# Self attention of a four layer block: the order of scores, constant products, transposes, maxima and copies, and four small steps on GpSimd

## The chip, the cores and the metric

One core of a Trainium2 chip runs the whole program; the other cores are idle. The metric is device time in microseconds (us) of one execution. The engines are TensorE (PE), VectorE (DVE), ScalarE (ACT), GpSimd (POOL) and SyncE (SP), which only issues transfers here.

## The reference

Four layers follow each other on tokens x of shape (4, 256, 256); each is a cross attention on a context of 64 positions and then an FFN block, both added to x. The FFN block of the third layer (called 2 in the kernel) begins with a self attention of its own, and that is the part the change touches. In short, with n the layer norm of x, and dropping biases and the rotation's tables:

```python
q, k, v = heads(rms(n) @ wq + bq), heads(rms(n) @ wk + bk), heads(rms(n) @ wv + bv)   # 16 heads of 16
q, k = rope(q, k)
scores = where(causal, einsum('bqhd,bkhd->bhqk', q, k) / 4, -inf)
attn = softmax(scores, axis=-1)
n = n + einsum('bhqk,bkhd->bqhd', attn, v) @ wo
h = rms(n)                                    # router, experts and shared FFN follow
x = x + n + ffn(h)
```

## The kernel before

x lies in SBUF as eight tiles of 128 tokens (two per batch), and so does n (`xn`). Every engine has its own written-out queue; semaphores tie them together (`s.p` is the exponentials, `s.pt_ps` the transposes, `s.pt` their copies, `s.mx` the maxima, `s.one` the inverses of the sums spread over a head's columns, `s.oneT_ps` their transposes, `s.o` the normalised context, `s.y_ps` its product with wo). `me.link` is an increment of VectorE's own semaphore followed by a wait for it.

The self attention is `pe_self`, `act_self`, `dve_self` and the second half of `pool_pre2`. It has 32 steps (`SA_STEPS`): eight query tiles (`bq`), and in each four steps of four heads. An even query tile sees 128 keys, an odd one 256. For a step t:

- `pe_scores(t)` (L2222) waits for the exponentials of step t-2, whose banks it takes over, and makes the mask (L2232) and the three f16 products (L2242) of four heads.
- `dve_maxima(t)` (L2102, L2106) reduces them to negated maxima; `act_self` (L2337) makes the exponentials with their sums, four instructions.
- `turned(t)` of `pe_self` (L2249) waits for the copy of step t-1, then for some steps issues products of constants whose result nobody reads (`pe_warm`, L306: three at t % 4 = 2, four at t = 1 and 4), then waits for the exponentials of t and transposes them (L2259, four or eight). All steps use the same two PSUM banks.
- `turned(t)` of `dve_self` (L2353) copies them to SBUF.
- `values` (L2276) multiplies them with v, two steps at a time.

Once per query tile there are the reciprocals of the sums (L2359), their spreading to 256 columns (L2360), the transposes of that (`sums_transposed`, L2284), its evacuation on ScalarE (L2329), the multiplication of the context by it (`normalised`, L2367), the product with wo (`project`, L2290), the addition to n (L2373), the addition of n to x (L2374) and the sum of squares (L2375). The layer norm of one tile (`dve_normed`, L1899) is also one VectorE instruction of this loop. GpSimd does nothing in the loop and two powers (L1857) behind it.

The order of the main loops is:

```python
# pe_self                          # dve_self
turned(t)                          reciprocals if t % 4 == 3
pe_scores(t + 2)                   turned(t)
values(t - 2) if t even            dve_maxima(t + 2)
sums_transposed if t % 4 == 0      dve_normed if t % 4 == 1
project if t % 4 == 3              normalised if t % 4 == 2, added if t % 4 == 0
# act_self: exponentials(t); sums_evacuated if t > 4 and t % 4 == 1
```

Of the kernel before, what the change touches and what calls it, by code (L numbers as in the profile page):

```python
# [16 lines left out]
ALU, ACT, AX = mybir.AluOpType, mybir.ActivationFunctionType, mybir.AxisListType  # L17

P = 128
D = 256  # L20
KT = D // P
B, S, L = 4, 256, 64
NT = B * S // P
QT = S // P
# [68 lines left out]
def build(nc, d, out):  # L93
    ctx = ExitStack()
    with ctx:
# [98 lines left out]
        def bank(n, k=1):  # L194
# [18 lines left out]
               2: Sems("att2", "bt_ps bt e_ps e m_ps mh m f_ps f c_ps c dt_ps dt q s")}  # L213
        pre = [Sems("pre0", "fold_ps fold ms r z zT_ps zT biased y_ps ssq rr z2 z2T_ps h low"),
               Sems("pre1", "h low logit e t"),
               Sems("pre2", "hT z zT_ps ms r qkv biased copied qr qrT_ps qhi qT s mx p pt_ps pt one oneT_ps oneT v pv o y_ps x2 "
                    "ssq rr z2 z2T_ps h low logit e t"),
               Sems("pre3", "h low logit lg t")]
        ffn = Sems("ffn", "up0 up1 dn0 dn1 up_hi up_lo dn_hi dn_lo parts gates_ps gates rows gate0 gate1 "
# [1444 lines left out]
        def dve_ffn(n, begun=0):  # L1664
            dve, s, f = nc.vector, ffn, FFNS[n]
            LAG = lag(n)

            def low(st):
                dve.wait_ge(s.hi, f.steps0 + place(n, st) + 1)
                if gated(n, st):  # L1670
                    dve.tensor_tensor(hid_part(n, 1, st), m_b[:, st % PRODUCTS, :], hid_part(n, 0, st), ALU.subtract).then_inc(s.lo, 1)  # L1671
                else:
                    dve.scalar_tensor_tensor(hid_part(n, 1, st), m_b[:, st % PRODUCTS, :], plain_down_scale(n, st), hid_part(n, 0, st),
                                             ALU.mult, ALU.subtract).then_inc(s.lo, 1)

            for st in range(f.steps + LAG - 2):
                c, h, due = st // 2, st % 2, finished(n, st)
                if len(due) == 2:
                    if due[0] % 2 == 0:
                        dve_dn_lo(n, due[0] // 2)  # L1680
                    low(due[0])
                if begun <= st < f.steps:
                    dve_front(n, st)
                if h == 0 and 2 <= c + 1 < f.tiles:
                    dve_up_lo(n, c + 1)
                if due and due[-1] % 2 == 0:
                    dve_dn_lo(n, due[-1] // 2)
                if st < f.steps and product_first(n, st):
                    dve.wait_ge(s.t, f.steps0 + st + 1)
                    dve.scalar_tensor_tensor(m_b[:, st % PRODUCTS, :], m_t[:, h, :], 1.0, m_a[:, h, :], ALU.add, ALU.mult).then_inc(s.prod, 1)  # L1690
                if due:
                    low(due[-1])
                if n == 0:
                    dve_routed(own["dve"], st)
            for i in range(NT):
                dve.wait_ge(s.y_ps, NT // 2 * n + i // 2 + 1)
                dve.scalar_tensor_tensor(x[:, i, :], PS[:, 4 + i // 2, (i % 2) * D:(i % 2 + 1) * D],
                                         UNDOWN if n else p0_down[:, i:i + 1], x[:, i, :], ALU.mult, ALU.add).then_inc(ffn_x, 1)
                if n == 2:
                    dve_stats(2 * n + 2, i)  # L1700
            if n == 1:
                for i in range(NT):
                    dve_stats(2 * n + 2, i)
# [542 lines left out]
        def pe_self():  # L2246
            pe, s = nc.tensor, pre[2]

            def turned(t):  # L2249
                b, q, j0, keys = sa_part(t)  # L2250
                if t:
                    pe.wait_ge(s.pt, t)
                    if t % SA_OF_Q == 2 or t in (1, 4):
                        pe_warm(3 if t % SA_OF_Q == 2 else 4, 2)
                pe.wait_ge(s.p, t + 1)
                for e in range(2):
                    for a in range(2):
                        for k in range(q + 1):
                            ins = pe.transpose(PS[:, 2 + e, (a * (q + 1) + k) * P:(a * (q + 1) + k + 1) * P],  # L2259
                                               sa_p[:, t % 2, e, a * keys + k * P:a * keys + (k + 1) * P], ident[:])  # L2260
                ins.then_inc(s.pt_ps, 1)

            def values(t):

                b, q, j0, keys = sa_part(t)
                bq = t // SA_OF_Q
                pe.wait_ge(s.pt, t + 2)
                if j0 == 0:
                    pe.wait_ge(s.v, b + 1)
                    if bq >= 2:  # L2270
                        pe.wait_ge(s.x2, bq - 1)
                for a in range(2):
                    for k in range(q + 1):
                        for j in range(j0, j0 + 4):
                            out_ps = PS[32 * (j % 4):32 * (j % 4) + 32, 6 + q, (j // 4) * P:(j // 4 + 1) * P]
                            ins = pe.matmul(out_ps, sa_vm[b][:, k, j, a, :, :].rearrange("p e c -> p (e c)"),  # L2276
                                            turned_part(t + (j - j0) // 2)[:, j % 2, (a * (q + 1) + k) * P:(a * (q + 1) + k + 1) * P],
                                            start=(a == 0 and k == 0), stop=(a == 1 and k == q))
                ins.then_inc(s.pv, 2)

            def sums_transposed(bq):
                pe.wait_ge(s.one, bq + 1)
                for g in range(G):
                    ins = pe.transpose(PS[:, 6 + bq % QT, D + g * P:D + (g + 1) * P], sa_one[:, g * P:(g + 1) * P], ident[:])  # L2284
                ins.then_inc(s.oneT_ps, 1)

            def project(bq):
                pe.wait_ge(s.o, bq + 1)
                for g in range(G):
                    ins = pe.matmul(PS[:, 6 + bq % QT, 0:D], sa_oT[:, bq % QT, g, :], p2_wo[:, g, :], start=(g == 0), stop=(g == G - 1))  # L2290
                ins.then_inc(s.y_ps, 1)

            for t in range(1, SA_AHEAD):
                pe_scores(t)
            for t in range(SA_STEPS):
                turned(t)
                if t + SA_AHEAD < SA_STEPS:
                    pe_scores(t + SA_AHEAD)
                if t and t % 2 == 0:
                    values(t - 2)  # L2300
                if t and t % SA_OF_Q == 0:
                    sums_transposed(t // SA_OF_Q - 1)
                if t >= SA_OF_Q and t % SA_OF_Q == 3:
                    project(t // SA_OF_Q - 1)
            values(SA_STEPS - 2)
            sums_transposed(B * QT - 1)
            pe_warm(6, 2)
            project(B * QT - 1)

        def pool_values(me):  # L2310
# [4 lines left out]
            for i in range(NT):  # L2315
# [5 lines left out]
                if k == QT - 1:  # L2321
                    ins.then_inc(s.v, 1)

        def act_self():
            act, s = nc.scalar, pre[2]

# [4 lines left out]
            for t in range(SA_STEPS):  # L2331
                b, q, j0, keys = sa_part(t)
                act.wait_ge(s.mx, t + 1)
                for e in range(2):
                    for a in range(2):
                        h = 2 * (j0 + e) + a
# [8 lines left out]
        def dve_self(me):  # L2345
# [8 lines left out]

            def reciprocals(bq):
                dve.wait_ge(s.p, SA_OF_Q * (bq + 1))
                if bq:
                    dve.wait_ge(s.oneT_ps, bq)
                me.link(dve, dve.reciprocal(small[:, bq % QT, 2, :], small[:, bq % QT, 1, :]))  # L2359
                dve.tensor_copy(sa_one.rearrange("p (h c) -> p h c", h=H), over(small[:, bq % QT, 2, :], 2, HD)).then_inc(s.one, 1)  # L2360

            def normalised(bq):
# [7 lines left out]
            def added(bq):  # L2370
                dve.wait_ge(s.y_ps, bq + 1)
                dve.wait_ge(ln.xn, 5 * NT + bq + 1)
                me.link(dve, dve.tensor_tensor(xn[:, bq, :], xn[:, bq, :], PS[:, 6 + bq % QT, 0:D], ALU.add))  # L2373
                dve.tensor_tensor(x[:, bq, :], x[:, bq, :], xn[:, bq, :], ALU.add).then_inc(s.x2, 1)  # L2374
                ins = dve.scalar_tensor_tensor(p2_junk, xn[:, bq, :], 1.0, xn[:, bq, :], ALU.mult, ALU.mult,  # L2375
                                               accum_out=p2_ssq[:, bq:bq + 1])
                me.link(dve, ins)
# [9 lines left out]
            for t in range(1, SA_AHEAD):  # L2387
                dve_maxima(t)
            for t in range(SA_STEPS):
                if t % SA_OF_Q == SA_OF_Q - 1:  # L2390
                    reciprocals(t // SA_OF_Q)
                turned(t)
                if t + SA_AHEAD < SA_STEPS:
                    dve_maxima(t + SA_AHEAD)
                if t % SA_OF_Q == 1:
                    dve_normed(5, t // SA_OF_Q)
                if t >= SA_OF_Q and t % SA_OF_Q == 2:
                    normalised(t // SA_OF_Q - 1)
                if t >= 2 * SA_OF_Q and t % SA_OF_Q == 0:
# [37 lines left out]
        def pool_pre2():  # L2437
# [1 line left out]
            pool_ln(5)  # L2439
            me = own["pool"]  # L2440
            pool_values(me)
            for part in range(2):
                pool_pow(pre[2].ssq, part + 1, rms_r[:], rms_e[:], pre[2].rr, part)

        def dve_pre2():
            dve, s, me = nc.vector, pre[2], own["dve"]
# [265 lines left out]
```

## Time and profile before

| what | value |
|---|---|
| median of 3 runs | 1248.03 us (1244.47 to 1248.77) |
| the profiled execution | 1244.87 us |
| its span | 1242.8 us |
| PE, DVE, ACT, POOL busy | 95%, 74%, 41%, 32% |
| granted clock of TensorE over the span | 0.999 |
| self attention, scores of step 1 to last product with wo | 747.52 to 835.99 us |

The profile is one execution, taken by the hardware profiler. The span runs from its first to its last instruction. A record's length is start to end; instructions of one engine overlap, so the distance from start to start can be shorter than a record. Some matmul records are missing. "idle before <- releaser" in square brackets is the time in which the engine waited ahead of this record, and what ended the wait.

### The profile page before, as it was taken

Reading aid. Unit: us, or ns where it says so; the run is one execution under the profiler, and the core shown is the slowest. Engines: PE = TensorE matmul, PEld = TensorE weight load, DVE = VectorE, ACT = ScalarE, POOL = GpSimd, SP = SyncE. Lnnn points to the kernel's source line nnn. Section 1 sums busy time; section 2 is a strip of 40 time slices with the busy share of each in tenths; the row PEclk is TensorE's granted clock in tenths of the full one; section 3 lists DMA queues with packets and bytes.
Section 4 is the critical chain, followed back from the end, with each engine's and each line's share of the span. In section 5 each row is a group of like instructions: output and inputs, shape, how many; then the busy total and the mean of one; then the engine's idle time right before and its main releaser. Section 6 shows DMA issues by size and latency. Waiting matters only on the chain.

```text
span 1242.8 us, 21905 instructions
## 1 busy us (share of the span) xinstructions
PE 1179.6 (95%) x8530; PEld 768.3 (62%) x8559; DVE 917.5 (74%) x1718; ACT 505.3 (41%) x1141; POOL 393.2 (32%) x397
## 2 busy tenths in 40 slices
PE   6999999999999999999999989899999988999998
PEld 3664658999745555555766745564566665455556
DVE  3777976677677777778757798887866577777766
ACT  3523360111224333334453336653434353555553
POOL 1540215656305333334003330001534052433330
PEclk9999999999999999999999999999999999999999
DMA  4040141000065344443240000002532100533431
GB/s 150 2 161 22 49 148 39 1 1 2 5 218 161 119 119 119 116 117 105 94 150 1 3 15 1 2 1 60 168 128 92 61 19 1 151 113 113 123 119 56
DMA packets 41542, 97.18 MB, mean 78 GB/s; under 512 B 5446, under 2 KB 18246, under 8 KB 39392
## 3 DMA queue, kind: packets, MB, share of 16 engines
q1 hardware_dynamic: 41440, 95.79, 24.4%
q8 instruction: 68, 1.11, 0.4%
q14 instruction: 34, 0.28, 0.1%
HBM read 94.35 MB, written 1.42 MB: 77 GB/s over the span
## 4 chain that ended last, share of the span: by engine, by line
PE 76%; DVE 15%; issue 3%; ACT 3%; DMA 2%; POOL 1%; SPq 0%; DVEq 0%; ACTq 0%; POOLq 0%
PE PS L1461 9%; PE PS L1463 9%; PE PS L1462 9%; PE PS L1508 5%; PE PS L1510 5%; PE PS L1509 5%; PE PS L1074 3%; PE PS L1092 2%; PE PS L1271 2%; PE PS L306 2%; PE PS L1060 2%; PE PS L1062 2%; PE PS L1061 2%; PE PS L2259 1%; DVE small L577 1%
## 5 line engine op out<-in xcount | busy, mean ns | idle before, releaser
L1718 POOL TENSOR_TENSOR arena<-arena,m_g 128x512 f32<-128x512 f32 x142 | 196.7, 1406 | 351.6 <-DMA m_g<-gate_rows 344.1
L1461 PE MATMUL PS<-arena 128*128 128x512 f16 x608 | 230.7, 379 | 3.0 <-DVE arena L1656 2.4
L1462 PE MATMUL PS<-arena 128*128 128x512 f16 x608 | 230.7, 379 | 0.0
L1463 PE MATMUL PS<-arena 128*128 128x512 f16 x608 | 230.6, 379 | 0.0
L1508 PE MATMUL PS<-arena 128*128 128x256 f16 x608 | 166.3, 274 | 6.6 <-DVE arena L1671 5.0
L1510 PE MATMUL PS<-arena 128*128 128x256 f16 x608 | 166.3, 274 | 0.0
L1509 PE MATMUL PS<-arena 128*128 128x256 f16 x608 | 166.2, 273 | 0.0
L1611 ACT ACTIVATE arena<-PS 128x512 f32<-128x512 f32 x112 | 66.8, 597 | 226.6 <-PE PS L1463 219.9
L1659 DVE SCALAR_TENSOR_TENSOR arena<-arena,PS 128x512 f32<-128x512 f32 x112 | 76.8, 685 | 77.1 <-ACT arena L1611 75.9
L1671 DVE TENSOR_TENSOR arena<-arena 128x512 f16<-128x512 f32 x142 | 128.5, 909 | 2.2 <-ACT arena L1622 1.8
L1463 PEld LDWEIGHTS PS<-arena 128*128 128x128 f16 x608 | 59.5, 98 | 71.9 <-issue 0.3
L1461 PEld LDWEIGHTS PS<-arena 128*128 128x128 f16 x608 | 59.5, 98 | 63.8 <-DVE arena L1656 3.4
L1462 PEld LDWEIGHTS PS<-arena 128*128 128x128 f16 x608 | 59.5, 98 | 57.9 <-issue 0.2
L1145 POOL TENSOR_TENSOR arena<-arena 128x256 f32<-128x256 f32 x96 | 67.6, 726 | 79.4 <-DVE arena L1175 79.3
L1622 ACT ACTIVATE arena<-arena 128x512 f16<-128x512 f32 x142 | 87.0, 618 | 2.9 <-PE PS L1510 2.9
L1662 DVE TENSOR_TENSOR arena<-arena,PS 128x512 f32<-128x512 f32 x112 | 77.0, 687 | 12.6 <-DVE arena L1659 0.9
L1552 DVE SCALAR_TENSOR_TENSOR arena<-w_stage,arena 128x512 f16<-128x512 f32 x80 | 78.9, 988 | 6.3 <-ACT arena L1547 6.3
L1508 PEld LDWEIGHTS PS<-arena 128*128 128x128 f16 x608 | 59.5, 98 | 36.4 <-issue 8.8
L1509 PEld LDWEIGHTS PS<-arena 128*128 128x128 f16 x608 | 59.6, 98 | 16.9
L306 PE MATMUL PS<-causal_b,ident_b 128*128 128x512 bf16 x246 | 60.0, 379 | 7.2 <-DVE arena L2353 5.7
L1510 PEld LDWEIGHTS PS<-arena 128*128 128x128 f16 x608 | 59.6, 98 | 7.1
L2337 ACT ACTIVATE arena<-PS,arena 128x128 f32<-128x128 f32 (+1 forms) x128 | 52.0, 420 | 21.7 <-DVE arena L2106 21.5
(282 smaller groups left out, 2223.1 us busy)
## 6 DMA issues: line engine op xcount, KB each, us to landing
w_stage<-in_up SPq DMA_DIRECT2D x80, 256.0 KB, 3.0
m_g<-gate_rows SPq DMA_DIRECT2D x70, 256.0 KB, 4.1
arena<-in_heads SPq DMA_DIRECT2D x16, 1088.0 KB, 5.3
w_stage<-in_down SPq DMA_DIRECT2D x80, 128.0 KB, 2.1
m_g<-gate_rows SPq DMA_DIRECT2D x17, 512.0 KB, 4.0
m_g<-gate_rows SPq DMA_DIRECT2D x6, 448.0 KB, 3.9
m_g<-gate_rows SPq DMA_DIRECT2D x6, 384.0 KB, 4.1
m_g<-gate_rows SPq DMA_DIRECT2D x6, 320.0 KB, 4.1
```

Source lines behind the costliest of these rows:

```text
L306: nc.tensor.matmul(PS[:, free, :], ident_b[:], mask_lat, start=True, stop=True)
L1461: pe.matmul(to, w_hi, x_hi, start=(k == 0), stop=False)
L1462: pe.matmul(to, w_lo, x_hi, start=False, stop=False)
L1463: ins = pe.matmul(to, w_hi, x_lo, start=False, stop=(k == KT - 1))
L1508: pe.matmul(to, h_hi, w_hi, start=(c == 0 and i % 2 == 0), stop=False)
L1509: pe.matmul(to, h_hi, w_lo, start=False, stop=False)
L1510: ins = pe.matmul(to, h_lo, w_hi, start=False, stop=(last and i % 2 == 1))
L1552: nc.vector.scalar_tensor_tensor(up_w[:, c % 2, 1, :], up_in[:, c % 2, :], SPLIT, up_w[:, c % 2, 0, :], ALU.mult, ALU.subtract).then_inc(s ...
L1622: act.activation(hid_part(n, 0, st), m_b[:, st % PRODUCTS, :], ACT.Copy).then_inc(s.hi, 1)
L1662: dve.tensor_tensor(m_b[:, st % PRODUCTS, :], a, u_ps, ALU.mult).then_inc(s.prod, 1)
L1671: dve.tensor_tensor(hid_part(n, 1, st), m_b[:, st % PRODUCTS, :], hid_part(n, 0, st), ALU.subtract).then_inc(s.lo, 1)
L1718: pool.tensor_tensor(p, p, m_g[:, st // 2 % 2, st % 2, :], ALU.mult).then_inc(s.c, 1)
```

## The change

```diff
 # pe_self
             for t in range(SA_STEPS):
-                turned(t)
                 if t + SA_AHEAD < SA_STEPS:
                     pe_scores(t + SA_AHEAD)
+                turned(t)
 # values: PSUM banks of tile bq are free again
-                        pe.wait_ge(s.x2, bq - 1)
+                        pe.wait_ge(s.mixed, bq - 1)
 # act_self
                 act.wait_ge(s.mx, t + 1)
+                if t >= 2:
+                    act.wait_ge(s.pt_ps, t - 1)
 # dve_self
             def reciprocals(bq):
                 dve.wait_ge(s.p, SA_OF_Q * (bq + 1))
-                if bq:
-                    dve.wait_ge(s.oneT_ps, bq)
-                me.link(dve, dve.reciprocal(small[:, bq % QT, 2, :], small[:, bq % QT, 1, :]))
+                if bq >= 2:
+                    dve.wait_ge(s.one, bq - 1)
+                ins = dve.reciprocal(small[:, bq % QT, 2, :], small[:, bq % QT, 1, :])
+                if bq < B * QT - 1:
+                    ins.then_inc(s.inv, 1)
+                    return
+                me.link(dve, ins)
+                dve.wait_ge(s.oneT_ps, bq)
+                dve.wait_ge(s.one, bq)
                 dve.tensor_copy(sa_one.rearrange("p (h c) -> p h c", h=H), over(small[:, bq % QT, 2, :], 2, HD)).then_inc(s.one, 1)
             def added(bq):
-                me.link(dve, dve.tensor_tensor(xn[:, bq, :], xn[:, bq, :], PS[:, 6 + bq % QT, 0:D], ALU.add))
-                dve.tensor_tensor(x[:, bq, :], x[:, bq, :], xn[:, bq, :], ALU.add).then_inc(s.x2, 1)
+                dve.tensor_tensor(xn[:, bq, :], xn[:, bq, :], PS[:, 6 + bq % QT, 0:D], ALU.add).then_inc(s.mixed, 1)
+                dve.wait_ge(s.mixed, bq + 1)
             for t in range(SA_STEPS):
+                if t + SA_AHEAD < SA_STEPS:
+                    dve_maxima(t + SA_AHEAD)
                 if t % SA_OF_Q == SA_OF_Q - 1:
                     reciprocals(t // SA_OF_Q)
                 turned(t)
-                if t + SA_AHEAD < SA_STEPS:
-                    dve_maxima(t + SA_AHEAD)
-                if t % SA_OF_Q == 1:
-                    dve_normed(5, t // SA_OF_Q)
 # pool_pre2: the two powers are now inside pool_self
+        def pool_self():
+            pool, s = nc.gpsimd, pre[2]
+            def normed(i):
+                pool.wait_ge(ln.rstd, powers_before[5] + 1)
+                pool.tensor_scalar(xn[:, i, :], x[:, i, :], meanvar[:, i, 0:1], rstd[:, i:i + 1],
+                                   ALU.subtract, ALU.mult).then_inc(ln.xn, 1)
+            def spread(bq):
+                pool.wait_ge(s.inv, bq + 1)
+                if bq:
+                    pool.wait_ge(s.oneT_ps, bq)
+                pool.tensor_copy(sa_one.rearrange("p (h c) -> p h c", h=H), over(small[:, bq % QT, 2, :], 2, HD)).then_inc(s.one, 1)
+            def added(bq):
+                pool.wait_ge(s.mixed, bq + 1)
+                pool.tensor_tensor(x[:, bq, :], x[:, bq, :], xn[:, bq, :], ALU.add).then_inc(s.x2, 1)
+            normed(0)
+            for bq in range(B * QT - 1):
+                normed(bq + 1)
+                spread(bq)
+                if bq:
+                    added(bq - 1)
+            pool_pow(s.ssq, 1, rms_r[:], rms_e[:], s.rr, 0)
+            added(B * QT - 2)
+            pool_pow(s.ssq, 2, rms_r[:], rms_e[:], s.rr, 1)
+            added(B * QT - 1)
 # end of the FFN of layer 2, ahead of its additions to x
+            if n == 2:
+                dve.wait_ge(pre[2].x2, NT)
```

Two semaphores are new, `inv` and `mixed`. No arithmetic changes.

## Rows read from the trace of the kernel before

**Rows 1.** Stretches: length, busy us of PE, PEld, DVE, ACT, POOL; granted clock, DMA.
```profile
747.52:763.68 16.16, 15.01 (x134) 7.97 (x137) 12.01 (x16) 10.57 (x50) 0.00 (x0) 1.00 0.01 2
785.12:806.57 21.45, 19.67 (x226) 12.64 (x227) 19.04 (x33) 14.38 (x66) 0.00 (x0) 1.00 0.01 2
828.01:836.00 7.99, 6.69 (x93) 4.70 (x92) 6.68 (x18) 2.31 (x9) 1.33 (x1) 1.00 0.01 2
```
**Rows 2.** Waits in 785.12 to 806.57 us: total us, times, longest us.
```profile
ACT arena L2337 <- DVE arena L2106: 5.5, 5, 1.6
...
PE PS L306 <- DVE arena L2353: 1.5, 2, 1.1
```

**Rows 3.** Timeline of TensorE: start us, length us, instruction.
```profile
784.69 0.59 PE L306 MATMUL PS<-causal_b,ident_b 128*128 128x512 bf16 x2 [1.09 <-DVE arena L2353]
785.12 1.04 PE L2259 MATMUL PS<-ident,arena 128*128 128x128 f32 x8
785.99 0.38 PE L2232 MATMUL PS<-causal_b,ident_b 128*128 128x256 bf16 x2
...
786.74 1.08 PE L2276 MATMUL PS<-arena 128*32 128x128 f32 x32
787.75 1.09 PE L2259 MATMUL PS<-ident,arena 128*128 128x128 f32 x8
...
789.42 1.13 PE L2290 MATMUL PS<-arena 128*128 128x256 f32 x4
790.39 0.60 PE L2259 MATMUL PS<-ident,arena 128*128 128x128 f32 x4
790.83 0.38 PE L2232 MATMUL PS<-causal_b,ident_b 128*128 128x256 bf16 x2
...
801.00 0.82 PE L2242 MATMUL PS<-arena 32*128 32x512 f16 x6
...
802.08 0.65 PE L2276 MATMUL PS<-arena 128*32 128x128 f32 x16
802.65 0.44 PE L2284 MATMUL PS<-ident,arena 128*128 128x128 f32 x2
802.93 1.04 PE L2259 MATMUL PS<-ident,arena 128*128 128x128 f32 x8
```

**Rows 4.** Timeline of VectorE.
```profile
788.88 1.22 DVE L2353 COPY arena<-PS 128x1024 f32<-128x1024 f32 x1
790.02 0.68 DVE L2106 TENSOR_REDUCE arena<-PS 128x4 f32<-128x512 f32 x1
...
792.74 0.43 DVE L2374 TENSOR_TENSOR x<-x,xn 128x256 f32<-128x256 f32 x1
...
794.75 0.40 DVE L1899 TENSOR_SCALAR xn<-x,meanvar,rstd 128x256 f32<-128x256 f32 x1
...
798.42 0.29 DVE L2360 COPY arena<-small 128x256 f32<-128x256 f32 x1
```

**Rows 5.** Timeline of ScalarE.
```profile
785.57 0.47 ACT L2337 ACTIVATE arena<-PS,arena 128x256 f32<-128x256 f32 x1 [1.59 <-DVE arena L2106]
...
787.29 0.21 ACT L2337 ACTIVATION_READ_ACCUMULATOR arena<-PS,arena 128x1 f32 x1
788.05 0.37 ACT L2337 ACTIVATE arena<-PS,arena 128x128 f32<-128x128 f32 x1 [0.55 <-DVE arena L2106]
...
789.34 0.21 ACT L2337 ACTIVATION_READ_ACCUMULATOR arena<-PS,arena 128x1 f32 x1
...
793.05 0.38 ACT L2329 ACTIVATE arena<-PS 128x256 f32<-128x256 f32 x1 [0.81 <-PE PS L2284]
```

**Rows 6.** Min/median/max ns of a line: L1867, L1899 near 81 us, L1659.
```profile
L1867 POOL TENSOR_TENSOR arena<-xn,arena x8: 722/910/916, 81.6 to 87.6; 128x256 f32<-128x256 f32 x8
L1899 DVE TENSOR_SCALAR xn<-x,meanvar,rstd x8: 406/952/959, 81.1 to 86.1; 128x256 f32<-128x256 f32 x8
L1659 DVE SCALAR_TENSOR_TENSOR arena<-arena,PS x112: 673/686/690, 101.9 to 1223.0; 128x512 f32<-128x512 f32 x112
```

More of the change, by code:

```diff
@@ L215, in build @@
                Sems("pre1", "h low logit e t"),
-               Sems("pre2", "hT z zT_ps ms r qkv biased copied qr qrT_ps qhi qT s mx p pt_ps pt one oneT_ps oneT v pv o y_ps x2 "
+               Sems("pre2", "hT z zT_ps ms r qkv biased copied qr qrT_ps qhi qT s mx p pt_ps pt inv one oneT_ps oneT v pv o y_ps mixed x2 "
                     "ssq rr z2 z2T_ps h low logit e t"),
@@ L2441, in pool_pre2 @@
             pool_values(me)
-            for part in range(2):
-                pool_pow(pre[2].ssq, part + 1, rms_r[:], rms_e[:], pre[2].rr, part)
+            pool_self()
         def dve_pre2():
```

## The prediction, made before the changed kernel was run

> **What bounds the kernel now.** The page's shares say only that TensorE is nearly always busy. The change touches one stage, the self attention of the third FFN layer, so the view that counts is busy time by stretch [rows 1]. The stage runs from 747.52 us (scores of step 1) to 835.99 us (last product with wo), 88.47 us or 7% of the span of 1242.8. It settles into a period of eight steps (two query tiles, one with 128 keys, one with 256): three of them, 21.44 to 21.45 us (one stands). In a period TensorE is busy 19.7 us, VectorE 19.0, ScalarE 14.4, GpSimd 0. Two engines are close to full and a third is in a loop with them, so what decides is who waits for whom. The waits [rows 2]: ScalarE waits 5.5 us a period for maxima, TensorE 1.5 us for copies of transposed probabilities (that wait stands in front of the constant products, L306).
>
> For the replay below I read occupied times as start to next start. TensorE [rows 3]: eight transposes 0.87 (785.12 to 785.99; elsewhere up to 1.0, I take 0.93), four transposes 0.44 (790.39; up to 0.59 elsewhere, I take 0.48), scores of a 128 key step 0.75 (785.99 to 786.74), of a 256 key step 1.07 to 1.08 (801.00 to 802.08), values 1.01 (786.74) or 0.57 (802.08), sums 0.27 (802.65), product with wo 0.97 (789.42), three constant products 0.65 (three at 0.215, the first of the three at 784.47 has no record). Over a period: 4 x 0.93 + 4 x 0.48 + 4 x 1.07 + 4 x 0.75 + 2 x 1.01 + 2 x 0.57 + 2 x 0.27 + 2 x 0.97 + 2 x 0.65 = 19.85. So TensorE stands idle 1.6 us a period; before steps 14 and 22 about 1.1 us of it in one piece. VectorE [rows 4]: copies and maxima 1.14 (256 keys) or 0.61 (128). ScalarE [rows 5]: a step's exponentials take 1.93 us from the first start to the last end for 256 keys (785.57 to 787.50) and 1.50 for 128 (788.05 to 789.55), eight records each, the first and the last of which stand; the evacuation of the sums (793.05) holds the queue 0.28 us. From a producer's end to the consumer's start: 0.04 us to VectorE, 0.03 to ScalarE, 0.06 to 0.13 to TensorE. Putting the queues of lines 2293 to 2304, 2331 to 2343 and 2387 to 2400 in their order with these times gives a period of 21.48 us and a stage of 88.46 us, against 21.44 and 88.47 in the trace; so I use the same table for the new order.
>
> **What GpSimd takes over.** Per tile VectorE loses the normalisation (0.41 us record, 0.33 occupied), the spreading of the inverses (0.29, some 0.21 to 0.34 with the wait behind the reciprocal) and the addition to x (0.43, 0.35 occupied) [rows 4]: 0.9 to 1.0 us a tile, 7 to 8 us in all. GpSimd gets 8 normalisations, 7 spreads (the eighth stays on VectorE), 8 additions. Its price here is not shown; the nearest row is its addition of 128x256 in the first FFN block, 0.72 to 0.92 us [rows 6]; a normalisation or a broadcast copy may differ. I take 0.9, as bounds 0.7 and twice the row's median, 1.8. Even at 1.8 us the seven spreads come in time: the reciprocal stands at step 4n+3, the transposes of the sums follow a step later, some 3 us on, and GpSimd has three instructions in 10 us. So GpSimd's own work costs nothing while it hides in that slack; without it each spread would add its length in front of a sums transpose. Its last additions stand behind the power that VectorE waits for and are needed only at the end of the FFN, so the new wait for x2 there costs 0. Keeping the old order and moving this work alone, the table gives 87.4 us: only 1.0 us of the 7 to 8 comes off, since TensorE and the loop through it stay.
>
> **The new order.** Scores(t+2) now stand before constants and transposes(t) on TensorE, maxima(t+2) before copy(t) on VectorE, and exponentials(t) wait for transposes(t-2) (the p buffer was guarded by the order before). No instruction is added or taken on TensorE, so its 19.85 us a period remain; only waits can change. Three things follow.
> 1. Scores(t+2) wait for exponentials(t). In the old order the transposes of t, which want the same exponentials, and ahead of them the constant products stood there; the products filled the wait. Now TensorE stands still in front of the scores with everything behind it, and the constant products come afterwards, in series.
> 2. The evacuation of the sums stands on ScalarE's queue ahead of exponentials 4n+2. It already waits 0.81 us for the transposes of the sums [rows 5]. ScalarE is now further ahead of TensorE, so this wait sets its pace. One period from transposes(14) = 0: values and scores(17) to 2.69, transposes(15) to 3.62, product to 4.59, scores(18) 5.34, transposes(16) 5.82, values 6.83, sums to 7.10 (result 7.27); evacuation 7.30, exponentials(18) 7.58 to 9.08; scores(19) and transposes(17) are done at 8.33, so scores(20) wait from 8.33 to 9.21: 0.88 idle. Constants to 10.93, then without a wait transposes(18), values, scores(21), transposes(19), product, scores(22), transposes(20), values and sums to 17.33. Evacuation again, exponentials(22) 17.81 to 19.74; TensorE ends transposes(21) at 19.33 and starts scores(24) at 19.87: 0.54 idle, to 20.62. Maxima(23) start at 18.86 behind the squares, copy(21) at 20.00 and ends at 21.22, so the constants of step 22 start at 21.28: 0.66 idle; transposes(22) at 21.93.
> 3. The period is thus 21.93 us: idle 2.08 against 1.6 before.
>
> **Sum.** Steps 1 to 6 take 18.20 against 16.16 us [rows 1]: 0.75 is scores(8), now ahead of that point, the rest waits, chiefly 1.22 us in front of scores(3), where the four constants of step 1 used to stand. The three periods: 3 x 21.93 - 64.33 = +1.5. The end from step 30: 7.77 against 7.98, -0.2 (the power, the tokens and the last product are in the same order). Together +2.0 + 1.5 - 0.2 = +3.3 us. Behind the stage the ten constants ahead of the logits (ten at 0.215) hide the 0.35 us that the missing addition saves; should they not, the end comes 0.35 us earlier. Contention adds 0 to 2.7 us (next part), I take 0.7: **+4 us**, 0.3%. Changing each time of the table by 0.1 us moves the difference by at most 0.8, so the bounds without contention are +2 and +5.
>
> The profiled execution took 1244.87 us (span 1242.8 and 2.1 around it), so it would be 1248.9; the median of the three runs is 1248.03, 3.2 above it, which would give 1252. I take the middle, 1250.5.
>
> **Contention.** VectorE's normalisation takes 0.40 us in this stage, where GpSimd is idle [rows 4], and mostly 0.95 us in the first FFN block, where GpSimd adds beside it; products with a PSUM operand stay at 0.69 us at the most, GpSimd busy or not [rows 6]. The copies, maxima and the multiplications by inverses read PSUM and are not stretched; the squares (L2375) and reciprocals read SBUF only. Stretched by 0.5 us each, they lengthen the period in the table: 1.5 us over the stage for the squares, 2.7 with the reciprocals and a GpSimd at 1.3 us.
>
> The Trainium skill (Advanced Engine Details and Errata, VectorE Performance Modes) says that VectorE's second SBUF port is shared with GpSimd and that the two block each other in 2-port modes. By that rule the squares, which read one tensor twice, and not the PSUM copies, would pay, as the trace's 0.69 against 0.95 us suggests; it is the third rival below.
>
> **Rivals.**
> - *The waits go and the relief comes through.* If exponentials run ahead as the order means them to, only TensorE's work is left. Ceiling: all idle of the stage, some 7.8 us; 1.0 is what the relief gives alone. Against it: the evacuation on ScalarE's queue. Time -1 to -6, say -3: 1246.5. Chance 0.14, of which 0.05 passes 0.5%.
> - *Nothing to be seen*, -1 to +2: relief and waits cancel, for instance if transposes behind scores run 0.05 us shorter (32 x 0.05 = 1.6). 1248.5. Chance 0.2.
> - *Clearly slower.* GpSimd stretches VectorE's SBUF instructions on the path copy(21), maxima(23): +2.7 on the +3.3, and transposes behind a score product cost 0.05 more each (+1): +7, 1253.5. It decides when squares take over 0.8 us. Chance 0.24.
> - *TensorE's clock drops.* Granted clock is 1.00 (2.4 GHz) in all stretches [rows 1], with pauses up to 1.1 us; the longest new one is 1.95 us, before step 30. A stretch of 3 us at 1.2 GHz would cost 1.5 us. Chance 0.02, in the slower share.
>
> **The numbers.** 0.5%, 6.2 us, is about what a measurement here can tell from no change. The forecast (+2 to +6) holds 0.40; with the second rival and the first's small part the middle has 0.69; faster 0.05; slower 0.26. The range takes the runs' own spread (1244.5 to 1248.8) with -3 and +10: 1242 to 1259.
>
> **What would show it.** Right: a period of about 21.9 us; TensorE waiting 0.9 us in front of scores for exponentials, twice a period; the wait in front of L306 down from 1.1 to about 0.7; ScalarE waiting over 1 us for the sums (0.8 before); VectorE under 17.5 us busy a period; L2375 at 0.42 to 0.9 us. Wrong: a period under 21.2 us, TensorE's waits in front of scores under 0.3 us, or PSUM copies over 1.3 us.

## The result, and the profile after

The changed kernel takes 1250.22 us (median of 17, 1245.77 to 1254.18) against 1245.34 us for the kernel before in the same comparison (1241.97 to 1248.77). The ratio is 1.0035 with a 95% interval of 1.0024 to 1.0046, so +3.0 to +5.7 us. That is a real loss and a small one: within the half per cent that was called no change, and near the forecast of +4.

The profile after has a span of 1248.7 us. Its lines are two further down from L2106 on (maxima L2108, masks L2234, scores L2244, transposes L2261, values L2278, sums L2286, product L2292); copies are L2386, exponentials L2370, the evacuation L2360, the squares L2414. Busy time by stretch, columns as in [rows 1]: steps 1 to 6, one period from transposes(14) to transposes(22), the end from transposes(30), and the whole stage.

```profile
747.59:767.45 19.86, 17.68 (x144) 9.09 (x145) 12.42 (x15) 12.33 (x58) 1.60 (x2) 0.91 0.00 1
789.19:810.92 21.73, 20.05 (x227) 12.70 (x226) 17.11 (x26) 14.17 (x68) 5.12 (x6) 1.00 0.01 2
832.66:840.89 8.23, 6.75 (x93) 4.68 (x91) 5.99 (x15) 0.50 (x3) 2.04 (x2) 1.00 0.01 2
747.59:840.89 93.30, 83.79 (x906) 51.53 (x906) 69.15 (x107) 55.37 (x257) 17.78 (x21) 0.98 0.01 2
```

Against [rows 1]: 19.86 us for 16.16, 21.73 for 21.45, 8.23 for 7.98, and the stage 93.30 for 88.47, +4.8. VectorE has been relieved as intended (17.1 us busy in a period, 19.0 before) and the period is 0.3 us longer all the same. The granted clock of the first stretch is 0.91, which was 1.00; more on that below.

Where TensorE stands still in a period is in its timeline, which answers to [rows 3].

```profile
796.06 0.44 PE L2286 MATMUL PS<-ident,arena 128*128 128x128 f32 x2
...
797.09 0.66 PE L2261 MATMUL PS<-ident,arena 128*128 128x128 f32 x4
798.38 0.82 PE L2244 MATMUL PS<-arena 32*128 32x512 f16 x6 [0.63 <-ACT arena L2370]
...
807.36 1.04 PE L2261 MATMUL PS<-ident,arena 128*128 128x128 f32 x8
808.75 0.39 PE L2234 MATMUL PS<-causal_b,ident_b 128*128 128x256 bf16 x2 [0.34 <-ACT arena L2370]
...
810.27 0.82 PE L306 MATMUL PS<-causal_b,ident_b 128*128 128x512 bf16 x3 [0.70 <-DVE arena L2386]
810.92 1.04 PE L2261 MATMUL PS<-ident,arena 128*128 128x128 f32 x8
```

Three waits: scores(20) 0.63 us and scores(24) 0.34 us for exponentials, the constants of step 22 0.70 us for a copy, 1.67 us in all. The kernel before has three others in the period of [rows 3]:

```profile
794.52 0.59 PE L306 MATMUL PS<-causal_b,ident_b 128*128 128x512 bf16 x2 [0.42 <-DVE arena L2353]
...
800.00 1.06 PE L2259 MATMUL PS<-ident,arena 128*128 128x128 f32 x8 [0.27 <-ACT arena L2337]
...
806.13 0.59 PE L306 MATMUL PS<-causal_b,ident_b 128*128 128x512 bf16 x2 [1.10 <-DVE arena L2353]
```

A row of L306 with two products where three were issued lacks the record of one; that product's 0.22 us is then counted in the wait. So 0.42 stands for some 0.20 and 1.10 for some 0.88, and with 0.27 the waits before come to 1.35 us. The 0.3 us between 1.67 and 1.35 are the 0.3 us of the period. The waits for exponentials in front of scores are new; the one in front of the constants of the odd tile shrank by some 0.2 us, from 0.88 to 0.70. ScalarE's timeline shows what stands in front of the first, and answers to [rows 5].

```profile
796.54 0.38 ACT L2360 ACTIVATE arena<-PS 128x256 f32<-128x256 f32 x1 [1.64 <-PE PS L2286]
796.82 0.36 ACT L2370 ACTIVATE arena<-PS,arena 128x128 f32<-128x128 f32 x1
...
806.49 0.38 ACT L2360 ACTIVATE arena<-PS 128x256 f32<-128x256 f32 x1 [1.01 <-PE PS L2286]
806.77 0.47 ACT L2370 ACTIVATE arena<-PS,arena 128x256 f32<-128x256 f32 x1
```

ScalarE waits 1.64 and 1.01 us for the transposes of the sums (0.81 and 0.7 before) and starts exponentials(18) right behind the evacuation; their end releases scores(20).

GpSimd's share, its timeline over one tile and at the end of the stage:

```profile
792.95 0.40 POOL L2338 COPY arena<-small 128x256 f32<-128x256 f32 x1 [5.09 <-DVE small L2392]
796.28 0.96 POOL L2342 TENSOR_TENSOR x<-x,xn 128x256 f32<-128x256 f32 x1 [2.93 <-DVE xn L2412]
797.23 1.21 POOL L2331 TENSOR_SCALAR xn<-x,meanvar,rstd 128x256 f32<-128x256 f32 x1
...
838.84 0.72 POOL L2342 TENSOR_TENSOR x<-x,xn 128x256 f32<-128x256 f32 x1
```

The spread inverses are ready at 793.35, 2.7 us ahead of their transposes at 796.06. At the end of the stage the addition of tile 6 runs beside four VectorE instructions that read and write SBUF only (VectorE's timeline, after and before):

```profile
838.98 1.53 DVE L2424 TENSOR_SCALAR arena<-xn,rms_r 128x256 f32<-128x256 f32 x4 [0.74 <-POOL rms_r L1859]
```
```profile
834.46 1.14 DVE L2385 TENSOR_SCALAR arena<-xn,rms_r 128x256 f32<-128x256 f32 x4 [0.39 <-POOL rms_r L1857]
```

### The profile page after: what moved, and what is told of

Same layout as the page of the kernel before. It is cut to its first block, busy times and chain, and to the rows that moved or that the text cites. A ratio compares the mean times of both kernels' runs of the same rounds, so it can differ in the third digit from the quotient of the medians.

```text
span 1248.7 us, 21977 instructions
## 1 busy us (share of the span) xinstructions
PE 1183.5 (95%) x8559; PEld 769.2 (62%) x8559; DVE 909.2 (73%) x1695; ACT 505.0 (40%) x1141; POOL 411.7 (33%) x420
## 4 chain that ended last, share of the span: by engine, by line
PE 76%; DVE 15%; issue 3%; ACT 2%; DMA 2%; POOL 1%; SPq 0%; DVEq 0%; ACTq 0%; POOLq 0%
PE PS L1461 9%; PE PS L1463 9%; PE PS L1462 9%; PE PS L1508 5%; PE PS L1510 5%; PE PS L1509 5%; PE PS L1074 3%; PE PS L1092 2%; PE PS L306 2%; PE PS L1271 2%; PE PS L1060 2%; PE PS L1062 2%; PE PS L1061 2%; DVE small L577 1%; PE PS L404 1%
## 5 line engine op out<-in xcount | busy, mean ns | idle before, releaser
L1659 DVE SCALAR_TENSOR_TENSOR arena<-arena,PS 128x512 f32<-128x512 f32 x112 | 76.8, 686 | 80.4 <-ACT arena L1611 79.1
L1671 DVE TENSOR_TENSOR arena<-arena 128x512 f16<-128x512 f32 x142 | 122.1, 864 | 1.7 <-ACT arena L1622 1.0
L1552 DVE SCALAR_TENSOR_TENSOR arena<-w_stage,arena 128x512 f16<-128x512 f32 x80 | 82.8, 1037 | 5.3 <-ACT arena L1547 5.2
L306 PE MATMUL PS<-causal_b,ident_b 128*128 128x512 bf16 x275 | 67.2, 383 | 4.0 <-DVE arena L2386 4.0
L2370 ACT ACTIVATE arena<-PS,arena 128x128 f32<-128x128 f32 (+1 forms) x128 | 51.9, 424 | 20.0 <-DVE arena L2108 10.4
```

The lines of the kernel that those rows point to most:

```text
L306: nc.tensor.matmul(PS[:, free, :], ident_b[:], mask_lat, start=True, stop=True)
L1552: nc.vector.scalar_tensor_tensor(up_w[:, c % 2, 1, :], up_in[:, c % 2, :], SPLIT, up_w[:, c % 2, 0, :], ALU.mult, ALU.subtract).then_inc(s ...
```

## The experiments

Twelve runs. Stage lengths below are from scores(1) to the last product with wo, periods from one reciprocal of an odd tile to the next odd one's in the middle of the stage; medians and ratios are over the whole program, against runs of the kernel before on the same chip. Where TensorE's clock fell within the stage, the table says so; such a stage is longer for that alone.

| run | stage us | period us | ratio to before, interval |
|---|---|---|---|
| before | 88.47 | 21.44 | 1 |
| changed | 93.30 (with clock fall) | 21.74 | 1.0035 (1.0024 to 1.0046) |
| changed, second profile | 91.69 | 21.74 | one run |
| order only | 93.86 (with clock fall) | 22.07 | 1.0040 (1.0026 to 1.0053) |
| GpSimd only | 87.86 | 21.11 | 0.9995 (0.9981 to 1.0008) |
| evacuation later | 89.57 | 21.03 | 1.0008 (0.9990 to 1.0026) |
| changed, no constants | 91.86 (clock at half for 14 us and for 3.4 us) | 20.53 | 0.9982 (0.9963 to 1.0001) |
| four p buffers | 91.69 | 21.74 | 1.0048 (1.0031 to 1.0064) |
| first wait filled | 91.68, twice | 21.73 | 1.0016 (1.0004 to 1.0027) |
| addition behind powers | 91.29 | 21.73 | one run |
| before, no constants | 87.80 | 21.38 | 1.0028 (1.0015 to 1.0041) |
| together, new order | 84.98 | 19.84 | 0.9959 (0.9947 to 0.9971) |
| together, old order | 85.29 | 20.38 | 0.9982 (0.9968 to 0.9995) |

**The order alone.** The kernel before with these hunks of the change only:

```diff
 # pe_self
-                turned(t)
                 if t + SA_AHEAD < SA_STEPS:
                     pe_scores(t + SA_AHEAD)
+                turned(t)
 # act_self
+                if t >= 2:
+                    act.wait_ge(s.pt_ps, t - 1)
 # dve_self: maxima ahead of reciprocals and copies
```

> The kernel before with the new order alone (scores before constants and transposes, maxima before copies, the wait of the exponentials for the transposes); GpSimd takes nothing over. Theory A (the order makes the loss: TensorE waits in front of the scores, constants come in series; GpSimd's share is a small gain): slower than the whole change, stage about 93 to 95 us against 88.5 before and 93.3 with the whole change, period about 22.3 us, so +5 to +7 us (+0.4 to +0.55%). Theory B (the GpSimd work makes the loss through late inverses or shared ports): about as before, +-1 us, period 21.4.

Stage 93.86, period 22.07: the loss is in the order. A period has 0.63 and 0.35 us in front of scores and, less a missing record, 0.8 in front of the constants, with VectorE busy 19.0 us in it.

```profile
809.58 0.39 PE L2232 MATMUL PS<-causal_b,ident_b 128*128 128x256 bf16 x2 [0.35 <-ACT arena L2339]
811.42 0.59 PE L306 MATMUL PS<-causal_b,ident_b 128*128 128x512 bf16 x2 [1.01 <-DVE arena L2355]
...
833.49 0.59 PE L306 MATMUL PS<-causal_b,ident_b 128*128 128x512 bf16 x2 [2.18 <-DVE arena L2355]
...
835.11 1.94 PE L2276 MATMUL PS<-arena 128*32 128x128 f32 x32
```

The last two rows show a fall of the clock inside this stage: behind the wait before step 30 the clock is at half from 834.6 to 838.0 us, and a `values` that takes 1.08 us elsewhere takes 1.94. At half speed for 3.4 us TensorE loses at most 1.7 us, so I estimate 92.2 us at the least for the stage without the fall, and only the period can be held against the forecast of 22.3.

**GpSimd's share alone.** The changed kernel with the order of before:

```diff
 # pe_self
-                if t + SA_AHEAD < SA_STEPS:
-                    pe_scores(t + SA_AHEAD)
                 turned(t)
+                if t + SA_AHEAD < SA_STEPS:
+                    pe_scores(t + SA_AHEAD)
 # act_self
-                if t >= 2:
-                    act.wait_ge(s.pt_ps, t - 1)
 # dve_self: maxima behind copies again
```

> The changed kernel with the order of before on TensorE, ScalarE and VectorE; GpSimd keeps the normalisations, spreads and additions. Theory A: a little faster than before, period 21.1 us, stage 87.4 us, -1 us (-0.1%), and no fall of the clock near step 1. Theory B: it carries the loss, stage 91 to 93 us, +3 to +5 us.

A gain of 0.33 us a period and 0.6 us over the stage; over the whole program not to be told from none. Theory B is out. VectorE's busy time in the stage falls from 75.8 to 69.3 us, and almost all of these 6.5 us were slack.

**The evacuation one step later.**

```diff
-                if t > SA_OF_Q and t % SA_OF_Q == 1:
+                if t > SA_OF_Q and t % SA_OF_Q == 2:
                     sums_evacuated(t // SA_OF_Q - 1)
```

> The changed kernel; ScalarE evacuates the sums one step later, behind exponentials 4n+2 instead of ahead of them. Theory A (this queue place is what TensorE waits for in front of scores(t+2)): the two waits for exponentials in a period go, period 21.1 us against 21.74, stage 2 to 2.6 us shorter than with the change, so +2 us against before (+0.15%). Rival (the wait of the exponentials for the transposes, or the exponentials themselves, set the pace): period stays within 0.15 us of 21.74.

The period falls to 21.03 us and the stage by 2.1, from the 91.69 of the profile without a clock fall to 89.57. Its timelines of ScalarE and TensorE, at the same step:

```profile
793.07 0.39 ACT L2360 ACTIVATE arena<-PS 128x256 f32<-128x256 f32 x1
794.37 0.37 ACT L2370 ACTIVATE arena<-PS,arena 128x128 f32<-128x128 f32 x1 [0.91 <-DVE arena L2108]
```
```profile
793.46 0.66 PE L2261 MATMUL PS<-ident,arena 128*128 128x128 f32 x4
794.05 0.82 PE L2244 MATMUL PS<-arena 32*128 32x512 f16 x6
...
806.17 0.59 PE L306 MATMUL PS<-causal_b,ident_b 128*128 128x512 bf16 x2 [1.44 <-DVE arena L2386]
```

The evacuation now waits for nothing (no bracket), the scores follow the transposes without a pause, and both waits for exponentials are gone. What is late next is copy(21), some 1.2 us in front of the constants (1.44 in a row that lacks one record). One queue place on ScalarE cost 0.7 us of the period, all that the new order had lost there: GpSimd's share alone, in the old order, has 21.11.

The stage keeps a loss: 89.57 us against 87.86 in the old order. So of the 3.8 us that the order costs (91.69 - 87.86) the evacuation's place is 2.1. The rest lies in the first steps. From scores(1) to the first reciprocal (L2392 and its like) it is 8.09 us in the old order and 10.36 in the new one, with the evacuation in either place; behind the last period the new order gives 0.7 us back.

**Without the constants of the loop**, in both kernels:

```diff
                     pe.wait_ge(s.pt, t)
-                    if t % SA_OF_Q == 2 or t in (1, 4):
-                        pe_warm(3 if t % SA_OF_Q == 2 else 4, 2)
```

> The changed kernel without the constant products inside the loop of 32 steps (their results are never read). Theory A (in the new order they stand in series with the waits): period down by the whole of 2 x 0.65 us to 20.5 to 20.7 us, stage 6 us shorter, against before -1.5 to -3 us. Rival 1 (they still fill waits, as in the old order): period falls by 0.3 us at the most. Rival 2 (they hold the clock): the granted clock falls under 0.95 in the loop and the stage grows.

> The kernel before without the constant products inside the loop of 32 steps (their results are never read). Theory A (in the old order they stand in a wait and cost next to nothing; in the new order the same edit took 1.2 us off a period): period 21.3 us against 21.44, -0.1 us, stage 87.3 us if the clock holds. Rival (they cost their length in either order): period 20.2 us, stage 83 us.

The same edit takes 1.21 us off a period in the new order (21.74 to 20.53) and 0.06 in the old (21.44 to 21.38). So the constants stood in a wait before, and stand in series after: theory A on both counts. The first of the two also shows the price. In its profile the clock is at half from step 1 to step 5, in the first three rows below; the fourth, one period later on, shows it back at full speed. It falls once more at 832.2 us, behind the wait before step 30.

```profile
753.60:757.00 3.40, 3.40 (x19) 1.83 (x16) 1.63 (x3) 2.20 (x12) 0.00 (x0) 0.51 0.01 2
757.00:763.00 6.00, 6.00 (x39) 2.58 (x38) 3.50 (x5) 3.12 (x13) 1.00 (x2) 0.50 0.01 3
763.00:767.50 4.50, 4.50 (x34) 2.77 (x32) 2.45 (x2) 1.56 (x8) 0.59 (x1) 0.52 0.00 0
784.17:804.71 20.54, 18.86 (x221) 12.03 (x220) 17.06 (x28) 14.17 (x66) 5.12 (x6) 1.00 0.01 2
```

The profiled execution was this kernel's slowest (1252.45 us; the other eleven lie between 1240.17 and 1245.34). My expectation of -1.5 to -3 us fits the median, -2.3. The stage of that profile is 1.4 us shorter than with the first profile of the change and not 6, so there the rival of the clock holds. Its mean clock is 0.990, that of the other eleven runs 0.996 or more.

The second one did not go as its stage says: the stage is 0.67 us shorter and the program 0.28% slower. In its profile the clock is low far behind the stage, in code that the edit leaves alone:

```profile
1060.00:1080.00 20.00, 19.86 (x90) 8.96 (x89) 13.47 (x17) 10.35 (x19) 6.70 (x5) 0.93 0.51 141
1080.00:1100.00 20.00, 16.90 (x90) 9.56 (x88) 14.28 (x17) 8.17 (x16) 11.07 (x8) 0.83 0.46 139
```

The kernel before has one such place in its profile (1080 to 1100 us, clock 0.91). A clock of 0.91 over 20 us is 1.8 us of TensorE's time, so falls of this kind come to 5 us or so in the one profile and to 1.8 in the other. It is not this profile alone: 11 of the 12 runs without constants have a mean clock of 0.997 or less, and 3 of the 17 runs of the kernel before on the same chip. So the slower median goes with a lower clock. Why leaving out constants near 750 us should lower the clock at 1060 and 1080 us is not settled.

**Four buffers for the exponentials.** `sa_p` gets two more buffers, in the space of `sa_r` and `sa_b`, free by then:

```diff
-                if t >= 2:
-                    act.wait_ge(s.pt_ps, t - 1)
+                if t >= 4:
+                    act.wait_ge(s.pt_ps, t - 3)
```

> The changed kernel with four buffers for the exponentials instead of two, so that they wait for the transposes of step t-4 and no longer of step t-2. Theory A (ScalarE's waits for transposes, 7.2 us in three periods, are slack; the place of the evacuation sets the pace): period stays at 21.74 us within 0.1. Rival (the new wait of the exponentials is what holds TensorE's scores up): period 21.0 to 21.2 us, the two waits for exponentials in front of scores gone.

Period 21.74 and stage 91.69, both as with two buffers. ScalarE's waits for transposes of probabilities are gone, and its wait for the sums grew from 2.6 to 3.3 us a period (waits of one period, total, times, longest):

```profile
ACT arena L2365 <- PE PS L2291: 3.3, 2, 2.3
```

TensorE waits as with two buffers, 0.64, 0.35 and, less the missing record, 0.70 us:

```profile
796.40 0.82 PE L2249 MATMUL PS<-arena 32*128 32x512 f16 x6 [0.64 <-ACT arena L2375]
...
806.77 0.39 PE L2239 MATMUL PS<-causal_b,ident_b 128*128 128x256 bf16 x2 [0.35 <-ACT arena L2375]
...
808.52 0.59 PE L306 MATMUL PS<-causal_b,ident_b 128*128 128x512 bf16 x2 [0.92 <-DVE arena L2391]
```

The new wait of the exponentials costs nothing in the stage.

**The first wait, and the clock.** Four constants more, into a free bank:

```diff
                 turned(t)
+                if t == 0:
+                    pe_warm(4, 7)
```

> The changed kernel with four constant products more, behind the transposes of step 0 and into a bank not yet used, where TensorE waits 0.98 us for exponentials(1). Theory A (this new pause, close behind the 0.81 us one before scores(1), is what sometimes lets the granted clock fall to half near step 1): clock 1.00 between scores(1) and step 6 in the profile, transposes(6) 18.2 to 18.5 us after scores(1) against 19.86, and median 0 to 1.5 us under that of the whole change. Rival (the fall comes at random and does not depend on the pause): a fall is as likely as before; or the filled wait costs nothing and gains nothing in the median.

> The kernel with the first wait filled once more. Theory A: clock 1.00 behind scores(1) again, stage 91.7 us. A fall there would speak against the pause as its cause.

> The changed kernel itself once more, for another profile of the stretch behind scores(1), where the first profile shows the granted clock at half for 3.9 us. Theory A (a chance event that the pause in front of scores(3) allows): with or without a fall; stage 93.3 us with one, 91.7 without. Nothing tells which.

Both profiles with the fill have a clock of 1.00 and a stage of 91.68 us. The second profile of the changed kernel has no fall either, with the pause unfilled, and 91.69 us. So the fill itself is free (it stands in the wait) and the fall in the first profile cost 93.30 - 91.69 = 1.6 us. The row after the pause, and TensorE's clock in the 3.9 us behind it, in the first profile:

```profile
750.73 0.39 PE L2234 MATMUL PS<-causal_b,ident_b 128*128 128x256 bf16 x2 [0.98 <-ACT arena L2370]
...
751.49 1.89 PE L306 MATMUL PS<-causal_b,ident_b 128*128 128x512 bf16 x4
```
```profile
751.40:755.30 3.90, 3.90 (x19) 1.63 (x16) 1.38 (x2) 1.65 (x9) 0.00 (x0) 0.56 0.00 0
```

Of seven profiles with this pause unfilled two show a fall behind it (this one and the one without constants), of three with it filled none. That leans to the pause as a cause, and so does the median (1.0016 against 1.0035, intervals that just overlap, measured in separate comparisons). The mean clocks lean the same way: 0.997 or less in 2 of 12 runs with the fill, in 10 of 17 of the changed kernel and in 5 of 6 of the one with four buffers. A mean over the program doesn't tell where the clock fell, and the runs are from different chips; it is not proof.

**The addition behind both powers** on GpSimd's queue, one profile:

```diff
-            added(B * QT - 2)
             pool_pow(s.ssq, 2, rms_r[:], rms_e[:], s.rr, 1)
+            added(B * QT - 2)
```

> The changed kernel; GpSimd adds tile 6 to x behind both powers, so that it is idle while VectorE scales the first four tiles by the power. Theory A (the shared SBUF access stretches those four, 1.53 us against 1.14 before): they are 1.14 us again and the last product starts 7.9 us after transposes(30) instead of 8.23. Rival: 1.5 us as before, because something else slows them.

```profile
836.34 1.14 DVE L2424 TENSOR_SCALAR arena<-xn,rms_r 128x256 f32<-128x256 f32 x4 [0.74 <-POOL rms_r L1859]
```

1.14 us again, and the last product starts 7.84 us after transposes(30) (830.03 to 837.87) instead of 8.23.

**Together.** The evacuation later, the constants kept at t = 1, 2 and 4 only, and the addition behind the powers, in the changed kernel (there with the filled wait) and in the one with the old order:

```diff
-                    if t % SA_OF_Q == 2 or t in (1, 4):
+                    if t in (1, 2, 4):
                         pe_warm(3 if t % SA_OF_Q == 2 else 4, 2)
```

> New order and GpSimd's share, with the evacuation one step later, the constants of steps 6, 10, 14 and so on left out, the first wait filled and the addition of tile 6 behind the powers. Theory A: period 19.8 to 20.0 us, stage 84.6 to 85.5 us against 88.5 before, -3 to -4 us (-0.3%), clock 1.00. Rival (constants are needed for the clock): granted clock below 0.97 in the stage and a gain under 1 us.

> The order of before with GpSimd's share, the evacuation one step later, the same constants left out and the addition of tile 6 behind the powers. Theory A: period 20.3 us, stage 84.8 to 85.5 us, -3 to -3.6 us: without constants and with a free ScalarE queue the two orders are worth the same within 1 us. Rival (the new order is better as such once the evacuation is out of the way): e7 is ahead by 2 us or more.

Busy time by stretch, one period and the stage of each, new order first:

```profile
778.45:798.29 19.84, 18.62 (x221) 12.04 (x220) 17.07 (x28) 14.31 (x66) 5.12 (x6) 1.00 0.01 2
747.90:832.88 84.98, 77.66 (x886) 49.04 (x889) 68.60 (x107) 55.83 (x257) 17.11 (x20) 1.00 0.01 2
```
```profile
786.57:806.95 20.38, 18.95 (x221) 12.13 (x221) 17.15 (x28) 14.26 (x67) 5.12 (x6) 1.00 0.01 2
747.49:832.78 85.29, 78.12 (x883) 48.77 (x886) 68.97 (x107) 55.64 (x257) 17.10 (x20) 1.00 0.01 2
```

The periods are as forecast (19.8 to 20.0 and 20.3), and so are the stages. The new order has the shorter period by 0.54 us and pays most of it back in the first steps (10.36 us from scores(1) to the first reciprocal against 8.09): the stages differ by 0.3 us. Both beat the kernel before; the new order, at 1240.23 us against 1244.88, by 0.3 to 0.5%. Of the 2.5 us between the two medians the stage explains 0.3. By the stages theory A of the second text holds, by the medians its rival, and the rest of the 2.5 us is open. In the two profiles 2.2 us of it stand behind the stage, with a clock of 1.00 in both; but the two profiles of the kernel with the filled wait differ there by 2.7 us, also without a fall.

## Why the prediction was right, and where its terms were off

- **Sum of the stage.** Forecast: +3.3 us without contention and with the clock up. The profile whose clock stays up (second profile of the changed kernel) has 91.69 - 88.47 = +3.2, of which 0.4 is contention. So the waits were worth +2.8. Two errors in the parts nearly cancel, which is luck: the three periods lost 0.9 us and not 1.5, the end lost 0.25 where it was to gain 0.2. The measured +3.0 to +5.7 holds the forecast of +4 and leaves about a microsecond that the stage does not show.
- **The level.** The forecast of 1250.5 us came from three runs of the kernel before with a median of 1248.03, the measured 1250.22 from one of 1245.34. So the median was forecast 2.5 us above the kernel before and lies 4.9 above it; that the level fits to 0.3 us is luck.
- **The period** was put at 21.93 us and is 21.74. The mechanism is as described, wait for wait: in front of scores(20) 0.63 (0.88 forecast), of scores(24) 0.34 (0.54), of the constants 0.70 (0.66). The stretch from scores(20) to transposes(21) took 8.98 us where its terms gave 9.19: four times the scores of a 256 key step took 0.98 us (such as 801.11 to 802.09) and not 1.07. The evacuation as the cause, argued from 0.81 us of wait, is shown by moving it. One sign was read from unlike rows: the wait in front of L306, 1.1 us before, held a product without a record, so it fell from some 0.88 to 0.70 and the sign was weaker than it seemed.
- **Steps 1 to 6** were put at 18.20 us; 19.86 in the first profile, 1.6 of it the clock. In the second, transposes(6) start 18.24 us after scores(1) (745.67 to 763.91). Right, with the 0.98 us pause where 1.22 was forecast.
- **GpSimd's work hidden**: right. Its prices were 0.40, 0.96 and 1.21 us where I took 0.9 for each, inside the bounds.
- **Contention** was 0.4 us where I took 0.7, and above all mis-placed. I had it from squares and reciprocals in the loop. The squares kept their length: those at 796.23 us ran under GpSimd's addition of 796.28 and took 0.42 us. It is GpSimd's addition that was longer there, 0.96 us against 0.72 at the end of the stage. In the loop the squares start 0.05 us ahead of the addition, at the end the addition starts ahead of the scalings; that the later one pays fits both, and no run tests it. The 0.4 us came at the end, from four scalings beside one addition, 1.53 us for 1.14. I had written of those last additions that they cost nothing, since nobody waits for them; who runs beside them was the question. The Trainium skill (Advanced Engine Details and Errata, VectorE Performance Modes) ties the blocking to 2-port modes with source and destination in SBUF; the scalings meet that condition, and the trace agrees, with 1.53 us beside the addition and 1.14 without it (in which mode they ran no row shows). That the squares would pay, which I had drawn from the rule, was wrong here.
- **Constants in series**: right, 1.21 us a period in the new order and 0.06 in the old.
- **The clock** had a chance of 0.02. In the stage it fell in one of two profiles of the changed kernel, for 1.6 us, about the price given, but at step 1 and not at the 1.87 us pause before step 30, behind which it stayed at 1.00 in both. With the order alone and without constants it did fall behind that pause (some 1.9 us there too). So 0.02 was far too low, and this is the term of the sum that was missing. The kernel before had such a fall in its own trace, outside the stage (clock 0.91 from 1080 to 1100 us).
- **The rivals.** The waits did not go: 0.63 and 0.34 us in front of scores. "Nothing to be seen" did not come either, since the stage lost 3.2 us. The relief alone is 0.6 us in the stage (1.0 forecast, less the contention at the end). The clearly slower case did not come: its squares would have had to stretch.

## What to carry to other kernels

When work is issued earlier on one queue, look on the other queues for what stands ahead of the consumer it was meant to feed: here one evacuation held the exponentials and cost 0.7 us a period. (That its place was right for the old order is not shown: the old order with it one step later was run only together with other edits.) Filler that stood in a wait is work in series once the wait is in front of it; take it out, or move it with the wait, in the same edit. And an engine that is busy 89% of a period may give up 6.5 us of work in the stage for 0.6 us, if the loop through its neighbour stays.

## What was not expected of the hardware

- The granted clock of TensorE fell to half for stretches of 3.4 us (once 6.8, once 13.7), in unchanged code too, and in some profiles of a program but not in others. The places are few and recur. Behind the first 20 us the 14 profiles (twelve runs, before, changed) hold 23 falls, all near 361 us (2 profiles), 743 (4), 752 to 754 (2), 833 (2), 1000 to 1005 (2), 1057 to 1063 (5) or 1080 to 1086 (6); three profiles hold none. Near 743, 833, 1060 and 1080 us TensorE pauses for 1 us or more just there (1.06, 1.9, 2.4 and 2.5 to 3.1 us in profiles with a fall), but it pauses in the same way in profiles without one. A fall of 3.4 us takes 1.7 us of full speed work from TensorE.
- The falls are a part of the spread between runs of one kernel: of 81 runs of the kernel before, those with a mean clock of 1.000 take 1243.8 us on average (25 runs), those with 0.996 or less 1248.3 (15). Not all of it is clock, since stretches behind the stage differ by 2.7 us without a fall. A difference of 2 us between two kernels is therefore hard to assign, where their stages agree to 0.1 us between profiles that have no fall in them.
- Pauses of 0.98 us in front of scores(3) were followed by a fall in two of seven profiles; pauses of some 1.9 us before step 30, in the ten profiles of the new order, in two as well (the order alone, and without constants). Length of the pause alone does not tell.
